# Two of four tiles' pair vectors move to their rows by small ScalarE copies instead of identity matmuls

## The reference, cut to what matters

```python
e = jnp.stack([tbl_0[ids[:, 0]], ..., tbl_25[ids[:, 25]]], axis=1)      # 512 x 26 x 128
combined = jnp.concatenate([dense[:, None, :], e], axis=1)              # 512 x 27 x 128
interactions = jnp.einsum('bnd,bmd->bnm', combined, combined)
z = jnp.concatenate([dense, interactions[:, triu_i, triu_j]], axis=1)   # 128 + 351 pairs
h = jnp.concatenate([z, dense], axis=1)
h = jnp.maximum(h @ W_top1 + b_top1, 0.0)     # 607 x 512
h = jnp.maximum(h @ W_top2 + b_top2, 0.0)     # 512 x 256
y = h @ W_top3                                # 256 x 1
```

## Time and profile before

| | |
|---|---|
| Median of 3 runs | 109.49 us (109.1 to 110.28) |
| The profiled execution, its own time | 109.33 us |
| Its span in the profile | 107.4 us |
| TensorE matmuls busy | 98.3 us (92%) |
| VectorE busy | 86.0 us (80%) |
| GpSimd busy | 64.5 us (60%) |
| ScalarE busy | 64.4 us (60%) |

### The profile page before, as it was taken

How to read it: one execution, slowest core, us unless ns; L and a number is a source line. 1 busy time by engine, 2 the same in 40 slices (tenths; PEclk the granted TensorE clock), 3 DMA queues, 4 the chain that set the end, 5 groups by cost and what they waited for, 6 DMA issues and landing times.

```text
span 107.4 us, 3972 instructions
## 1 busy us (share of the span) xinstructions
PE 98.3 (92%) x1657; PEld 80.4 (75%) x1657; DVE 86.0 (80%) x255; ACT 64.4 (60%) x110; POOL 64.5 (60%) x68
## 2 busy tenths in 40 slices
PE   5969897997999899998999999999999997999991
PEld 2337576764766788877899887999798866998890
DVE  4799999999999999999999999999572436078121
ACT  5699989999999997809989474846300040001210
POOL 3577778777777778777777777777777700000000
PEclk9999999999999999999999999999999999999999
DMA  2999985747567847999782852112222110000000
GB/s 59 319 288 329 396 266 169 206 135 228 168 173 236 247 146 219 329 326 315 252 279 63 227 167 55 49 49 55 55 58 67 52 31 6 0 6 0 0 6 1
DMA packets 10575, 16.19 MB, mean 151 GB/s; under 512 B 2352, under 2 KB 6478, under 8 KB 10558
## 3 DMA queue, kind: packets, MB, share of 16 engines
q1 hardware_dynamic: 8398, 11.62, 34.0%
q0 software_dynamic: 2016, 4.13, 13.3%
q10 hardware_dynamic: 144, 0.19, 0.5%
HBM read 15.94 MB, written 0.00 MB: 148 GB/s over the span
## 4 chain that ended last, share of the span: by engine, by line
POOL 57%; issue 18%; PE 15%; DMA 6%; POOLq 1%; DVE 1%; DVEq 0%
POOL rows_sb L530 57%; PE h_ps L675 3%; DMA rows_sb<-in_tbl,ids_sb 3%; PE h_ps L650 3%; DMA ids_sb<-in_ids 2%; PE gram_ps L594 2%; PE h_ps L619 1%; PE turn_ps L650 1%; POOLq L293 1%; PE gram_ps L650 1%; PE turn_ps L619 1%; PE h_ps L658 1%; PE gram_ps L611 1%; PE turn_ps L594 1%; PE place_ps L611 0%
## 5 line engine op out<-in xcount | busy, mean ns | idle before, releaser
L530 POOL DMA_INDIRECT rows_sb<-in_tbl,ids_sb x63 | 63.6, 1009 | 20.9 <-issue 18.9
L571 PE MATMUL turn_ps<-onehot_sb,high_sb 128*128 128x512 f32 (+2 forms) x118 | 41.9, 367 | 3.5 <-DVE low_sb L807 1.4
L798 DVE TENSOR_SCALAR_CACHE_REDUCE onehot_sb<-lookup_ids_sb,first_sb 128x256 fp32r<-128x256 int16 (+2 forms) x79 | 43.6, 598 | 0.0
L572 PE MATMUL turn_ps<-onehot_sb,low_sb 128*128 128x512 f32 (+2 forms) x118 | 38.9, 342 | 0.0
L571 PEld LDWEIGHTS turn_ps<-onehot_sb,high_sb 128*128 128x128 f32 x118 | 22.2, 188 | 9.5 <-DVE low_sb L807 2.4
L572 PEld LDWEIGHTS turn_ps<-onehot_sb,low_sb 128*128 128x128 f32 x118 | 22.3, 189 | 1.6
L739 ACT ACTIVATE onehot_sb<-lookup_ids_sb,first_sb 128x512 fp32r<-128x512 int16 (+2 forms) x31 | 18.8, 621 | 2.3 <-PE turn_ps L572 2.2
L807 DVE TENSOR_TENSOR low_sb<-table_sb,high_sb 128x640 fp32r<-128x640 f32 (+1 forms) x26 | 19.4, 757 | 0.0
L729 ACT CAST high_sb<-table_sb 128x640 fp32r<-128x640 f32 (+1 forms) x26 | 17.0, 672 | 3.0 <-PE turn_ps L572 2.8
L594 PE MATMUL gram_ps<-feats 128*32 128x27 f32 x960 | 12.8, 196 | 1.1 <-DVE feats L701 0.4
L747 ACT ACTIVATE onehot_sb<-onehot_sb 128x768 fp32r<-128x768 f32 (+4 forms) x13 | 13.6, 1049 | 0.1
(11 more groups left out here) (53 smaller groups left out, 74.2 us busy)
## 6 DMA issues: line engine op xcount, KB each, us to landing
table_sb<-in_tbl SPq DMA_DIRECT2D x13, 256.0 KB, 3.5
table_sb<-in_tbl SPq DMA_DIRECT2D x7, 320.0 KB, 3.6
lookup_ids_sb<-in_lookup_ids SPq DMA_DIRECT2D x12, 128.0 KB, 2.4
table_sb<-in_tbl SPq DMA_DIRECT2D x6, 192.0 KB
rows_sb<-in_tbl,ids_sb POOLq DMA_INDIRECT x63, 3.3
w1p_sb<-in_w_pairs SPq DMA_DIRECT2D x1, 768.0 KB
w1d_sb<-in_w_dense SPq DMA_DIRECT2D x1, 512.0 KB, 6.3
w_sb<-in_w SPq DMA_DIRECT2D x1, 512.0 KB, 6.0
```

What stands on the lines that cost most here:

```text
L530: pool.indirect_dma_start(out=rows_sb[:, GATHERS.index((tile, slot)), :], out_offset=None, in_=tables[f], in_offset=bass.IndirectOffsetOnAxis(
L571: nc.tensor.matmul(bank, high_sb[0:rows, u % 2, c, :], picked, start=c == 0, stop=False)
L572: nc.tensor.matmul(bank, low_sb[0:rows, u % 2, c, :], picked, start=False, stop=c == CHUNKS[u] - 1).then_inc(chunk_used, 1)
L798: nc.vector.tensor_scalar(onehots(u, [c])[:, 0, :], lookup_ids_at(u), row_ids_sb[:, row:row + 1], None, ALU.is_equal, ALU.add, accum_out=m ...
```

## The change: what it does

Tiles 1 and 2 (`MOVED_TILES`) no longer use `place`. A new step `move` on ScalarE copies each of the four partition groups of `vecs` straight to each of the four row groups of `pairs`: sixteen copies of 32 partitions (31 for the last row group, because of the bias row) by 96 elements. Its last copy raises the semaphore `moved`, on which layer 1 and the next tile's merge wait in place of the old semaphores. Tiles 0 and 3 keep the matmuls and their copies.

All four orders are written anew. SP queues the weights of layer 1 (`w1d`, `w1p`) ahead of table 3, where `w1p` was between tables 9 and 10. On TensorE `layer2 0` comes after the lookups, and the turns of tile 3 stand between the steps of tiles 1 and 2.

```diff
+MOVED_TILES = (1, 2)
...
 PE_ORDER = """
...
-    0:2; layer2 0 1; turn 2 2; turn 2 3; lookup 12 2:10; place 1 0 32; gram 2 0 0; gram 2 0 1; layer1 1 0 4;
-    gram 2 1 0; gram 2 1 1; layer2 1 0; turn 3 0; turn 3 1; turn 3 2; place 2 0 32; layer2 1 1; turn 3 3; turn 3
-    4; gram 3 0 0; gram 3 0 1; layer1 2 0 4; gram 3 1 0; gram 3 1 1; layer2 2 0; layer2 2 1; dense1 3 0 1;
...
+    lookup 12 3:7; gram 1 1 1; lookup 12 7:9; turn 3 0; lookup 12 9; layer2 0 0; gram 2 0 0; layer2 0 1; gram 2
+    0 1; turn 3 1; layer1 1 0 4; gram 2 1 0; turn 3 2; gram 2 1 1; layer2 1 0; turn 3 3; layer2 1 1; turn 3 4;
+    gram 3 0 0; gram 3 0 1; layer1 2 0 4; gram 3 1 0; layer2 2 0; layer2 2 1; gram 3 1 1; place 3 0 16; dense1 3
...
 SP_ORDER = """
-    ids; table 0; id; table 1; table 2; dn; w1d; table 3; table 4; table 5; table 6; mask; table 7; table 8;
-    table 9; w1p; table 10; sm; w2; table 11; table 12
+    ids; table 0; id; table 1; table 2; w1d; dn; w1p; table 3; table 4; table 5; mask; sm; table 6; table 7;
+    table 8; table 9; table 10; w2; table 11; table 12
...
+        def wait_placed(engine, tile):
+
+            if tile in MOVED_TILES:
+                engine.wait_ge(moved, done("act", "move", tile))
+            else:
+                engine.wait_ge(placed_dve, done("dve", "place", tile, *place_parts(tile)[-1]))
+                engine.wait_ge(placed_act, done("act", "place", tile, *place_parts(tile)[-1]))
...
-                pe.wait_ge(placed_dve, tile + 1)
-                pe.wait_ge(placed_act, tile + len(place_parts(tile)))
+                wait_placed(pe, tile)
...
+            def move(tile):
+
+                act.wait_ge(merged, done("dve", "merge", tile, *gram_parts(tile)[-1]))
+                if tile >= 2:
+
+                    act.wait_ge(h1_done, tile - 1)
+                for q in range(QUADS):
+                    for to in range(QUADS):
+                        rows = min(NPAD, BIAS_ROW - to * NPAD)
+                        last = nc.scalar.copy(
+                            pairs[to * NPAD:to * NPAD + rows, :, tile % 2, q * GROUPS:(q + 1) * GROUPS],
+                            vecs[q * NPAD:q * NPAD + rows, 2 * to:2 * VECS:2 * QUADS, :])
+                last.then_inc(moved, 1)
...
-                    dve.wait_ge(place_done, done("pe", "place", tile - 1, *place_parts(tile - 1)[-1]))
+                    wait_vecs_read(dve, tile - 1)
```

More of the change, by code:

```diff
@@ L250 @@
[L250 removed]
+    distance 0 6; cast 0 0; cast 0 1; cast 1 0; distance 0 7; cast 1 1; onehot 0; distance 1 5:8; distance 2
+    6:8; copy lookup 0; onehot 1; dense; cast 2 0; copy turn 0 0; cast 2 1; copy lookup 1; onehot 2; distance 3
+    5; cast 3 0; cast 3 1; distance 3 6:8; cast 4 0; copy lookup 2; cast 4 1; onehot 3; distance 4 6:8; copy
+    turn 0 1; onehot 4; distance 5 5; cast 5 0; copy lookup 3; copy turn 0 2; distance 5 6:8; copy lookup 4;
+    cast 5 1; cast 6 0; cast 6 1; onehot 5; distance 6 8; copy turn 0 3; distance 6 9; copy turn 0 4; copy
@@ L251 @@
+    twin 3; distance 12 9; copy lookup 11; copy turn 2 3; onehot 12; copy lookup 12; move 1; copy turn 3 1; copy
+    turn 3 3; move 2; place 3 0 16; place 3 16 32; relu1 3 0 1; relu1 3 2 3
 """
 DVE_ORDER = """
-    onehot 0 0:4; low 0 0; low 0 1; onehot 0 4; low 1 0; onehot 0 5; onehot 1 0:5; low 1 1; onehot 2 0:4; low 2
-    0; low 2 1; onehot 2 4:6; low 3 0; low 3 1; onehot 3 0:5; onehot 4 0; low 4 0; onehot 4 1:3; low 4 1; onehot
-    4 3:6; onehot 5 0:2; low 5 0; onehot 5 2:5; low 5 1; onehot 6 0:3; low 6 0; onehot 6 3:6; copy turn 1 0; low
@@ L257 @@
-    6 1; onehot 6 6:8; onehot 7 0; low 7 0; onehot 7 1:4; low 7 1; onehot 7 4:7; onehot 8 0; merge 0 0 16;
-    onehot 8 1:4; low 8 0; onehot 8 4; merge 0 16 32; onehot 8 5; low 8 1; onehot 8 6:8; place 0 0 32; dense;
-    copy turn 1 2; onehot 9 0:4; low 9 0; onehot 9 4:7; low 9 1; low 10 0; onehot 10 0:2; copy turn 1 4; onehot
-    10 2:4; copy turn 2 0; relu1 0 0 4; low 10 1; onehot 10 4:8; onehot 11 0:2; low 11 0; onehot 11 2:6; low 11
-    1; onehot 11 6; low 12 0; onehot 12 0:6; low 12 1; onehot 12 6; merge 1 0 16; merge 1 16 32; copy turn 2 2;
@@ L262 @@
-    place 1 0 32; merge 2 0 16; layer3 0; relu1 1 0 4; merge 2 16 32; copy turn 3 0; copy turn 3 2; copy turn 3
-    4; layer3 1; place 2 0 32; relu1 2 0 4; merge 3 0 16; merge 3 16 24; merge 3 24 32; layer3 2; place 3 16 32;
-    relu1 3 1 2; relu1 3 3 4; layer3 3
+    onehot 0 0:4; low 0 0; onehot 0 4:6; low 0 1; low 1 0; onehot 1 0; low 1 1; onehot 1 1:5; onehot 2 0:4; low
+    2 0; onehot 2 4:6; low 2 1; onehot 3 0:2; low 3 0; onehot 3 2; low 3 1; onehot 3 3; low 4 0; onehot 3 4;
+    onehot 4 0:3; low 4 1; onehot 4 3:6; low 5 0; onehot 5 0:4; low 5 1; onehot 5 4; onehot 6 0:4; low 6 0;
@@ new lines @@
+    onehot 6 4:7; low 6 1; onehot 6 7; low 7 0; copy turn 1 0; onehot 7 0:3; low 7 1; onehot 7 3:7; low 8 0;
+    onehot 8 0:2; low 8 1; onehot 8 2:7; low 9 0; onehot 8 7; onehot 9 0:2; low 9 1; onehot 9 2; copy turn 1 2;
+    onehot 9 3:7; onehot 10 0; copy turn 1 4; merge 0 0 16; merge 0 16 32; onehot 10 1; copy turn 2 0; onehot 10
+    2; low 10 0; onehot 10 3; low 10 1; onehot 10 4:8; onehot 11 0:2; dense; onehot 11 2; place 0 0 32; onehot
+    11 3; low 11 0; low 11 1; low 12 0; low 12 1; onehot 11 4:7; onehot 12 0:3; copy turn 2 2; onehot 12 3:7;
@@ L603, in place @@
                 pe.wait_ge(merged, done("dve", "merge", tile, *last_merge))
-                if tile > 0 and first == 0:
-                    pe.wait_ge(placed_dve, tile)
-                    pe.wait_ge(placed_act, tile)
+                if first == 0:
+                    for before in [t for t in range(tile) if t not in MOVED_TILES][-1:]:
+                        wait_placed(pe, before)
                 for q in range(QUADS):
```

47 lines of the change are left out of this document (24 added, 23 removed).

## The result

The change makes the kernel slower. Its runs took 114.15 us in the median (113.66 to 115.69, 4 runs), against 109.32 (109.1 to 110.28) for the kernel before, which is a ratio of 1.041 with an interval of 1.032 to 1.050. The profiled run took 113.66 us with a span of 111.4, 4.0 more than the 107.4 before. The device has a slower state that lengthens some runs of any kernel by a few per cent: medians and ranges here are over all runs, and the ratios leave those runs out.

The account below looks back on a forecast made before the run. GpSimd's 63 indirect gathers were taken to bound the kernel to about 88.5 us, then TensorE's list. With everything hidden, span 107.4 + 0.0 and 1.9 around it gave 109.3, forecast 109.4 us, range 108.3 to 110.9.

Parts of the forecast that it names:

- rival (2): Move 2 becomes the wait, copies stepping by 0.28 us without overlap: 110.2 to 111.1 us, chance 0.14.
- sixteen copies at 0.15 us: ScalarE's move: 2.4 us plus 0.1 for the last copy's end, from bounds of 1.9 to 4.5 us.
- The line through the starts: ScalarE copy starts, 0.27 us at 256 elements and 0.64 at 640, extended to 0.12 us for a 96-element copy.
- the point from which move 2 decides: Ahead of layer 1 of tile 2: move 2 sets the time from 3.55 us for sixteen, 0.22 a copy.
- the cover of 2.2 us: TensorE's list from turn 3 1 to the last gather's landing: 2.2 us of late lookups, table loads or move 1 cost nothing.
- The lookups' end: VectorE's last one-hot still ends at 73.05 us; TensorE's last lookup matmul was taken to end at 74.9.
- Rival (5): Lookups end over 2.2 us late through the new orders and table 3: 110 to 112 us, chance 0.07.
- The end of the list: TensorE's reordered list behind 88.5 us: cost 0, bounds -0.1 to +0.3.
- 0.1 was said: Layer 2 of tile 2 after one half gram: relu1's 0.69 us against 0.65 of cover, so about +0.1.
- rivals (3): GpSimd's gathers fall worse on VectorE's low instructions, +0.6 to +1.7: 110.0 to 111.1 us, chance 0.15.
- (4): GpSimd's gathers fall better on VectorE's low instructions, -0.6 to -1.5: 107.9 to 108.8 us, chance 0.14.
- the 1 us that was allowed: GpSimd's gather chain: reordering VectorE's 26 low instructions gives nothing on average, but 1 us either way.

Follow-up runs that it names:

- probe: Kernel before with series of sixteen independent ScalarE copies appended behind its last use of the buffers; copies of the move's shape stepped by 0.173 us.
- split move: Changed kernel with each move split, ScalarE copying from partition groups 0 and 1, VectorE from 2 and 3, eight copies each; 110.25 us, single run.
- the old end: Changed kernel with moves split between ScalarE and VectorE, and the old order of steps behind layer 1 of tile 2; 110.09 us, ratio 1.006.
- lists alone: Changed kernel's new orders on all four engines, with tiles 1 and 2 placed by identity matmuls and copies, no moves; 110.40 us, ratio 1.008.
- half the copies: Changed kernel with only eight of the sixteen copies a move, half the pairs left at a memset value; 111.56 us, kernel before 109.80.
- moves alone: Kernel before with its old orders, the sixteen-copy moves replacing the places of tiles 1 and 2; 116.30 us, ratio 1.062.

## Why the prediction was wrong

It said 109.4 us, with a range to 110.9; the time is 114.15. The mechanism of its rival (2), move 2 becomes the wait because the copies step by 0.28, is the one that happened, at more than its price.

**The step that failed: sixteen copies at 0.15 us, 2.4 + 0.1 a move.** It measured 0.281 and 4.48, the upper bound of the range given, and move 2, which the sum had ready 1.1 us before layer 1 of tile 2 asked, held it for 2.34 us. The line through the starts of the earlier trace rows was right about copies of neighbours that keep their partitions (0.173 for this size, probe) and said nothing about copies that change them, which none of the rows did. The prediction named the shortness of the copies as the only thing that could break the line; it was not the shortness. It also took a value near the lower end for an operation that no row showed, in the one place where the bounds led to different verdicts: the point from which move 2 decides was put at 0.22 us a copy.

**The rival's price** was 110.2 to 111.1, since it let only move 2 be long. By the prediction's own times move 1 at 4.5 us ends at 76.1 + 4.5 = 80.6 where layer 1 of tile 1 comes at 79.4, and that was left to the cover of 2.2 us. That cover stands ahead of turn 3 4 and not ahead of move 2, whose start slips with whatever makes turn 3 3 late. Two delays drew on it at once. The last one-hot ended 1.6 us late (74.66, forecast 73.05), so move 1 began at 77.64, not 76.1, and with its extra 2 us ended at 82.12. Layer 1 began at 82.27 instead of 79.4, 2.9 late, and all behind it slipped: turn 3 3 ended at 89.33 (forecast 86.65), hence move 2 began at 89.77 (forecast 87.05). So move 1 delayed the start of move 2, which stood behind the copy of turn 3 3, and the two waits are one chain. An estimate from the same rows: had the moves taken 2.5 us from the same 77.64, move 1 would have ended at 80.1, before TensorE's 81.08, turn 3 4 would have begun at 90.03 - 1.19 = 88.84, move 2 would have run from 88.58 to 91.1 against a gram that ended at 90.9, and the whole would have cost 0.2 + 0.2 + 0.5, about 0.9 us. The split move lost 0.45 us (one run) and, with the old end, 0.7 (ten runs), which bears that out.

**The lookups' end** (forecast: unchanged). The start was 0.4 us later (first lookup matmul 7.33, 6.92 before) and TensorE's clock was low from 6 to 12 us in that profile; another run of the changed kernel had the clock at its upper level throughout and took 113.99, so the clock was not the cause of the loss. The lists alone end the last one-hot at 74.27 and the last lookup matmul at 76.77 too (77.05 in the changed kernel, 75.35 before). Rival (5) thus happened in part, just within the cover that it was given (77.05, forecast 74.9). One part of it can be read: VectorE, which before waited for nothing on this way, stands before low subtractions for casts of ScalarE, longest in the kernels that end latest (total wait, end of the last one-hot): none, 73.50 (split with the old end); 0.5, 73.75 (split); 0.9, 74.27 (lists alone); 1.0, 74.66 (changed); 1.6, 76.41 (half the copies). The rest is open.

**The end of the list** (forecast: 0.0, up to 0.3). It measured 0.47, all of it ahead of the pair matmuls of tile 3 (10.09 us behind the start of layer 1 of tile 2, 9.62 before). Layer 2 of tile 2 waits 0.19 us for relu1, where 0.1 was said. The merges held nothing: merge 3 24 32 ended at 102.79 and the second place began at 103.23. Most of the rest is that the two half grams, now apart, take 0.25 us more than together.

**What held.** The last gather was issued when it was before (84.98, before 85.03), so rivals (3) and (4) fell: in this profile the reordering of VectorE's 26 low subtractions did not move the chain. A spread of the 1 us that was allowed does occur: in the other traces from chips of this speed the last gather is issued between 84.31 and 86.13. And no kernel without the identity matmuls ran faster than the one before, as said.

**Sizes.** Lists +1.0 us; the moves on top of them 114.15 - 110.40, +3.8 us, from two chips on which the kernel before took 109.32 and 109.36; all of that goes with a move of half the length, which with the new lists is 0.45 us (one run), and with the old end 0.7 (ten), above the kernel before on its chip.

## What to carry to other kernels

Moving data between partition groups by many small ScalarE copies is priced by the copies' full duration, not by the step that a row of ordinary neighbours shows: sixteen cost 4.48 us where one identity pass on TensorE (0.87 us) and two copies side by side (0.47 and 0.56) did the same. Before such an operation is called hidden, look up not only who needs its result but who needs what is queued behind it on its engine, and follow its own delay into the start of the next one. Where no row shows an operation and the two bounds give different verdicts, the forecast should lean to the dearer bound, or the range reach it with all that follows.

## What the runs showed of the hardware

Neighbouring ScalarE copies of 96 elements a partition step by 0.173 us when source and target keep their groups of 32 partitions, and by 0.281 us, no less than their duration of 0.27, when either changes from one copy to the next; both ran as series of sixteen with no other engine computing, and the moves inside the kernel stepped by 0.281 too. The steps of series that keep their groups: 0.31 us for 256 elements, 0.42 for 384, under 0.1 for one, and 0.14 for 96 from PSUM. VectorE does eight of these copies, with changing groups, in 1.83 to 2.07 us, ScalarE in 2.24. TensorE's granted clock can fall behind a wait and make it dearer: in the kernel with the moves alone it was 1.00 up to each wait, 0.68 in the layer behind 2.33 us of waiting and 0.75 in the layer behind 3.22. It need not: behind the 2.34 us of the changed kernel it stayed at 1.00.
